# Four small moves on VectorE and GpSimd in the first seven steps of a gated cross-attention block

## The reference

```python
# x, ctx_2048: (16, 64, 256); 16 query heads in 4 groups, head dim 128
h = layernorm(x)
q = rope(rms_norm(h @ wq) * q_w)          # 16 heads
k = rope(rms_norm(h @ wk) * k_w)          # 4 kv heads, own tokens
v = h @ wv
k_ctx, v_ctx = rms_norm(ctx @ wk_ctx) * k_w, ctx @ wv_ctx
p = softmax(q @ [k_ctx, k].T / sqrt(128) + causal mask on the own tokens)
x = x + tanh(g_xattn) * ((p @ [v_ctx, v]) @ wo)
h = layernorm(x)
# gate_w, up_w, down_w are rounded to float8 e4m3 first; a value out of range becomes NaN
y = (silu((h @ gate8) * gate_scale) * ((h @ up8) * up_scale)) @ down8 * down_scale
x = x + tanh(g_ffn) * y
```

## Time and profile before

| | before |
|---|---|
| median of 3 runs | 308.26 (308.08 to 308.39) |
| the profiled execution, its own time | 308.09 |
| its span in the trace | 306.2 |
| granted TensorE clock | 1.0 of full speed throughout |
| PE busy | 292.1 (95%) |
| ScalarE busy | 234.6 (77%) |
| VectorE busy | 230.2 (75%) |
| GpSimd busy | 183.1 (60%) |

### The profile page before, as it was taken

One profiled execution on the slowest core, in us unless ns is written; L12 is line 12 of the kernel. 1 busy time (PEld: TensorE's weight loads), 2 busy tenths in 40 slices (PEclk: granted clock), 3 DMA queues, 4 the chain that ended last, 5 costly groups with the idle time before them and its releaser, 6 DMA issues.

```text
span 306.2 us, 6572 instructions
## 1 busy us (share of the span) xinstructions
PE 292.1 (95%) x2203; PEld 233.4 (76%) x2203; DVE 230.2 (75%) x497; ACT 234.6 (77%) x898; POOL 183.1 (60%) x181
## 2 busy tenths in 40 slices
PE   7898989998999999999999999999999999998876
PEld 3344656666877888888888888888888888886865
DVE  1668997989889977879865776777775865786553
ACT  2586789877889788898988779878888788877622
POOL 1446685677749597347945687547845686455230
PEclk9999999999999999999999999999999999999999
DMA  6999100000000010000000010000000000000001
GB/s 199 383 391 398 35 17 2 0 1 3 17 3 1 2 34 2 0 2 15 24 0 2 0 37 1 2 0 20 1 2 0 3 18 2 0 2 17 3 0 37
DMA packets 6722, 12.86 MB, mean 42 GB/s; under 512 B 800, under 2 KB 4256, under 8 KB 6688
## 3 DMA queue, kind: packets, MB, share of 16 engines
q1 hardware_dynamic: 6688, 12.43, 11.4%
HBM read 11.38 MB, written 1.05 MB: 41 GB/s over the span
## 4 chain that ended last, share of the span: by engine, by line
PE 70%; DVE 13%; ACT 6%; issue 4%; POOL 3%; DMA 2%; SPq 1%; DVEq 0%; POOLq 0%
PE ps_scores L714 8%; PE ps_attn L762 7%; PE ps_q L416 6%; PE ps_transposed L439 6%; PE ps_kv L416 6%; PE ps_y L460 6%; PE ps_ff L568 5%; PE ps_probs L439 5%; PE ps_y L453 4%; PE ps_q L421 3%; PE ps_ff L590 3%; PE ps_y L469 3%; PE ps_kv L421 3%; PE ps_kv L427 2%; DMA q_raw<-in_wq_dram 2%
## 5 line engine op out<-in xcount | busy, mean ns | idle before, releaser
L970 ACT ACTIVATE probs<-ps_scores,exp_bias,q_scale 128x128 f32<-128x128 f32 x128 | 56.9, 460 | 9.5 <-DVE exp_bias L1273 9.5
L1437 POOL TENSOR_TENSOR q_rot<-q_rot,q_sin 128x512 f32<-128x512 f32 x31 | 40.1, 1295 | 31.6 <-DVE q_sin L1139 31.5
L1517 POOL TENSOR_TENSOR probs<-probs,row_inv 128x512 f32<-128x512 f32 x32 | 36.2, 1132 | 18.4 <-DVE row_inv L1342 18.4
L1415 POOL TENSOR_TENSOR q_scale<-ssq_eps,minus_half 128x4 f32<-128x4 f32 x32 | 36.8, 1150 | 12.5 <-DVE ssq_eps L1312 11.5
L795 ACT ACTIVATE squares<-ps_q 128x128 bf16<-128x128 f32 x128 | 33.9, 287 | 8.9 <-DVE q_sin L1139 5.2
L714 PE MATMUL ps_scores<-kt,qt 128*64 128x128 f32 x512 | 34.4, 276 | 2.6 <-DVE ps_scores L1099 2.6
L762 PE MATMUL ps_attn<-pt,values 128*128 128x256 f32 x128 | 33.4, 383 | 0.0
L714 PEld LDWEIGHTS ps_scores<-kt,qt 128*64 128x64 f32 x512 | 28.0, 137 | 6.4 <-ACT qt L882 3.0
L946 ACT ACTIVATE pt<-ps_probs 128x512 f32<-128x512 f32 x32 | 19.2, 600 | 12.4 <-PE ps_probs L439 11.9
L1426 POOL TENSOR_TENSOR fuse_lo<-fuse,fuse_hi 128x256 fp32r<-128x256 f32 x21 | 15.3, 731 | 20.4 <-ACT fuse_hi L804 20.4
L795 ACT ACTIVATION_READ_ACCUMULATOR squares<-ps_q 128x1 f32 x128 | 27.4, 218 | 0.0
(11 more groups left out here) (199 smaller groups left out, 836.8 us busy)
## 6 DMA issues: line engine op xcount, KB each, us to landing
q_raw<-in_wq_dram SPq DMA_DIRECT2D x4, 512.0 KB, 8.5
o_raw<-in_wo_dram SPq DMA_DIRECT2D x4, 512.0 KB, 12.3
ctx_t<-in_ctx_dram SPq DMA_DIRECT2D x8, 128.0 KB, 2.6
out_dram<-x_sb SPq DMA_DIRECT2D x8, 128.0 KB, 1.7
stage<-in_gate_w_dram SPq DMA_DIRECT2D x2, 384.0 KB, 10.3
stage<-in_up_w_dram SPq DMA_DIRECT2D x2, 384.0 KB, 11.3
x_sb<-in_x_dram SPq DMA_DIRECT2D x1, 768.0 KB, 13.3
stage<-in_down_w_dram SPq DMA_DIRECT2D x2, 384.0 KB, 13.1
```

The lines of the kernel that those rows point to most:

```text
L970: last = nc.scalar.activation(probs[:, i, :], ps_s[:, i * P:(i + 1) * P], ACT.Exp, bias=exp_bias[:, i:i + 1], scale=q_scale[:, k % 2, i:i ...
L1415: return nc.gpsimd.tensor_tensor(dst, src, minus_half[:, 0:src.shape[1]], ALU.pow)
L1437: nc.gpsimd.tensor_tensor(q_rot[:, :, :], q_rot[:, :, :], q_sin[:, :, :], ALU.add)\
L1517: nc.gpsimd.tensor_tensor(probs[:, :, :], probs[:, :, :], row_inv[:, :].unsqueeze(2).broadcast_to([P, 4, P]), ALU.mult).then_inc(probs_rea ...
```

## The change

Four edits, all in the first seven steps; each instruction stays on its engine, and none is added or taken away.

1. VectorE: the peak pass of the first chunk (`out_of_range(0)`) leaves the end of step 0 and stands in step 1 between `k_var` (L1231) and `kn` (L1251), the normalized context keys of tile 1, which waits for GpSimd's `k_inv`.
2. GpSimd: `ln_inv` of tile 2 in step 2 stands behind the probabilities instead of ahead of them.
3. VectorE: `xn` of tile 2 in step 3 stands behind the bias of the exponential instead of ahead of the rotation.
4. VectorE: `x2n` of tile 0 leaves the start of step 6 and stands in step 5 ahead of the reciprocal, so also ahead of `down_rows`. Its second wait is for two turned `xn` tiles instead of three.

```diff
 # VectorE, one_step
-                if j == 2 and is_tile(u, m - 1):
+                if j == 2 and is_tile(u, m - 1) and at_step(u, k) != GROUPS + 2:
                     dve.wait_ge(x2_inv_ready, tile(u, m - 1) + 1)
...
-                if j == 3 and is_tile(u, m + 2):
+                if j == 3 and is_tile(u, m + 2) and at_step(u, k) != 3:
                     dve.wait_ge(ln_inv_ready, tile(u, m + 2) + 1)
...
+                if at_step(u, k) == 1:
+                    out_of_range(ROUND_AT[0])
+
                 if j == 1 and is_tile(u, m + 1):
                     dve.wait_ge(kc_inv_ready, tile(u, m + 1) + 1)
...
+                if at_step(u, k) == 3:
+                    dve.wait_ge(ln_inv_ready, tile(u, m + 2) + 1)
+
+                    if is_tile(u, m + 1):
+                        dve.wait_ge(xc_turned, tile(u, m + 1) + 1)
+                    if is_tile(u, m - 1):
+                        dve.wait_ge(x2_turned, tile(u, m - 1) + 1)
+                    nc.vector.tensor_scalar(xn[:, :], x_tile(u, m + 2), ln_mean[:, 0:1], ln_inv[:, 0:1],
+                                            ALU.subtract, ALU.mult).then_inc(xn_ready, 1)
...
+                if at_step(u, k) == GROUPS + 1:
+                    dve.wait_ge(x2_inv_ready, 1)
+                    dve.wait_ge(xc_turned, 2)
+                    nc.vector.tensor_scalar(x2n[:, :], x_tile(u, m - 1), x2_mean[:, 0:1], x2_inv[:, 0:1],
+                                            ALU.subtract, ALU.mult).then_inc(x2_ready, 1)
...
-                if at_step(u, k) in ROUND_AT:
+                if at_step(u, k) in ROUND_AT and at_step(u, k) != 0:
                     out_of_range(ROUND_AT[step(u, k)])
 # GpSimd, one_step
-                if j == 2 and is_tile(u, m + 2):
+                if j == 2 and is_tile(u, m + 2) and at_step(u, k) != 2:
                     pool.wait_ge(ln_var_ready, tile(u, m + 2) + 1)
...
                                             row_inv[:, :].unsqueeze(2).broadcast_to([P, 4, P]), ALU.mult).then_inc(probs_ready, 1)
+
+                if at_step(u, k) == 2:
+                    pool.wait_ge(ln_var_ready, tile(u, m + 2) + 1)
+                    if is_tile(u, m + 1):
+                        pool.wait_ge(xn_ready, tile(u, m + 1) + 1)
+                    inverse_root(ln_inv[:, :], ln_var[:, :]).then_inc(ln_inv_ready, 1)
```

## The result

The changed kernel takes 306.83 (median of 5 runs, 306.67 to 306.98) against 308.26 (308.08 to 308.39, 5 runs): 1.43 less, a ratio of 0.995 with a 95% interval of 0.9933 to 0.9967. Forecast was 306.9. The profiled execution took 306.83 itself, with a span of 305.0. By them the changed kernel has 306.78 (9 runs), and the kernel before 308.12 (16 runs) on the same chip, and 308.14 and 308.20 on the two others that were used.

What follows compares the result with a forecast made beforehand. TensorE, busy for 95% of the span, was taken as the bound, so only its waits could give time. 0.13 + 0.53 + 0.70 = 1.36 off 308.09 gave 306.73, forecast as a median of 306.9; 8-in-10 range 306.3 to 307.9.

Steps and rivals of the forecast that it cites:

- the row of step 9: Profile row before the change: a 4-column `k_var` begun 0.08 after GpSimd's probabilities took 0.99 and ended with them.
- The bound of 0.84 lost: Step 1, moved first peak pass: worst case, GpSimd's key root beside the reduce stretches from 1.01 to 1.98.
- the slack of the probabilities of step 3: Step 3: probabilities end at 51.62, TensorE turns them at 53.31; 1.69 of slack, of which 0.53 is used.
- The margin in GpSimd's order: Step 7: probabilities end at 79.97, TensorE wants them at 80.06, about 0.05 between; it fits by 0.04.
- The 0.17 that was added: Median of the three runs before lay 0.17 above the profiled execution, so 306.73 became a forecast of 306.9.
- The first rival: Steps 6 and 7: late probabilities take back the gain of the earlier `x2n`; 307.15 to 307.6; chance 0.20.
- the second: Step 1: the root is slowed or `kn` is late; 307.9 at worst, 307.3 in the middle; chance 0.06.
- the slower one: Steps 5 to 7: GpSimd's queue becomes the bound as roots, probabilities and `x2n` stretch; 308.8; chance 0.06.
- the moves don't reach the end: Step 2's head start is swallowed before step 5 and `x2n` isn't on the path; 308.2; chance 0.07.
- edit 4's upper bound of 0.88: Start of step 6: the most the earlier `x2n` could gain, TensorE's whole idle of 0.88; 0.70 was forecast.

Runs made afterwards that it cites:

- the longer root: The changed kernel with one more power of four columns on GpSimd, behind the probabilities of step 5, its result unused: 307.11, 0.33 more.
- the first probe: The changed kernel with one more power of one column on GpSimd, behind the probabilities of step 6, its result unused: 306.86.

## Why the prediction was right

- **Edit 1: 0.13 forecast, 0.14 in the trace, 0.13 by undoing it.** `k_var` fell into the probabilities as the row of step 9 said. The bound of 0.84 lost is out: the root beside the reduce took its 1.01. That also agrees with what the Trainium skill ("SBUF — State Buffer", section "Who interferes with whom") says of a reduce.
- **Edit 2: 0.53 forecast, 0.51 and 0.54 measured.** The probabilities had 0.16 of the subtraction before them (42.44 + 0.96 - 43.24) and took 1.05: it cost 0.03 at most. By the Trainium skill (same section), which has the loser blocked for the whole of the other's instruction, it would have been 0.16. In all three pairs shown some 0.12 of the remainder costs nothing (0.82 left for 0.70, 0.77 for 0.64, 0.16 for 0.03). Here the measurement decides for the price, and 0.53 was the right term. It doesn't show that the blocking is less than full: a printed end of VectorE can itself be late (`k_var` ends at 26.44 and the pass behind it starts at 26.35), and no run here tells a free remainder from a late printed end.
- **Edit 3: nothing on the path, right in the changed kernel.** But for an `xn` that isn't moved, the delay of 0.54 was taken to lie in the slack of the probabilities of step 3 (1.69), as in the expectation of the run without edit 3, and that was wrong. The shorter way runs over the bias, ScalarE's exponentials and squares, and VectorE's rotation of step 4, and has some 0.25 less room than the delay. Edit 3 is worth 0.24 in time once edits 1, 2 and 4 are there; so of the 0.54 of edits 2 and 3 together, edit 2 without edit 3 keeps 0.30 (307.02 against 307.32).
- **Edit 4: 0.70 forecast, 0.69 and 0.70 measured.** `x2n` took 0.41, and the later probabilities began at 68.82. The margin in GpSimd's order was put at 0.04; the longer root shows 0.05. What I called the probabilities of step 7 are those of step 6 by the code's count, which TensorE turns in step 7; the same slip put the first probe in the wrong place.
- **The sum: 1.36 forecast; 1.29 between the two profiled executions at the turn in step 7, and 1.35 from step 0 on, since in the changed kernel's the first loads came 0.06 later; 1.34 to 1.43 between medians.** The 0.17 that was added because the median lay above the profiled execution did not come again: the changed kernel's profiled execution is the median, 306.83, and between the profiled executions the times differ by 1.26. That the forecast of 306.9 is met within 0.07 is so in part by chance; each edit's share is met by its rows. The first rival (late probabilities eat edit 4) is excluded by edit 4's 0.70, the second by the root's 1.01, the slower one by rows that didn't stretch (1.02 and 0.76 for the two roots, 1.12 for the probabilities, 0.41 for `x2n`), and that the moves don't reach the end by TensorE's -1.26 at 257.
- **Idle and room.** I took TensorE to be free at 69.21. It is free some 0.16 earlier: behind four matmuls of this kind, printed as 1.88 long, the next group starts after 1.72 when nothing waits. So edit 4's upper bound of 0.88 was too small by this. The forecast didn't need it, because no edit filled TensorE's idle.

## What to carry to other kernels

Ask of each short wait whether VectorE or GpSimd is being held up by the other while it lasts: two passes that collide can be parted by order alone, and the moved instruction's own place matters less than what it keeps the other engine from starting. A pass that moves out of one collision must not land in another; fill a wait for GpSimd with a pass that left GpSimd's its time, such as here a reduce from one operand (the root took 1.01 beside it and 1.65 beside a subtraction). And follow a delay until it meets an idle that holds it on every engine, not only to the next wait of the bound one: here one of 0.5 went unseen for 16 us and came out at the next handover.

## What the runs showed of the hardware

- A GpSimd pass that begins while VectorE works on two SBUF operands is longer by what is left of that pass less some 0.12, whether it has 512 columns or 4: 0.70 for 0.82, 0.64 for 0.77, 0.03 for 0.16. Whether the 0.12 is free or comes from how ends are printed stays open.
- A 4-column VectorE pass (0.16) that begins beside a GpSimd pass of 512 or 768 columns ends with it: 0.92 long here, 0.89 and 1.54 beside the stores, and 0.17 and 0.15 once these were moved. The 128x768 reduce beside GpSimd's 4-column root cost neither anything (0.94 and 1.01).
- A printed idle of TensorE behind a group of matmuls is too small, by 0.16 behind the groups of 1.88 or 1.89 and by 0.07 behind the sixteen of the scores; the spacing of starts gives the room.
